# A 64-head long-convolution kernel on one core: outer-product tables, a new prologue, transposes ahead of the projection, and the projection in fp32r high and low parts

## The chip, the cores and the metric

The kernel runs on one core of a Trainium2 chip. A core has TensorE (matrix products, PE in the profile, its weight loads PEld), VectorE (DVE), ScalarE (ACT), GpSimd (POOL) and SyncE (SP, here the issuer of most transfers). Each engine works through its own instruction stream in order, and semaphores tie the streams together. The metric is the device time of one execution in microseconds; the median of several runs counts.

## What is computed

The input x is [128, 64, 1024]: batch, head, position. Cut to what matters:

```python
mask = arange(1024) < length[:, None]             # one length per batch row
u    = x * mask[:, None, :]
K    = 2 * einsum('hn,hnl->hl', Cs, exp(dtA[:, :, None] * arange(1024))).real   # 64 complex modes a head
y    = causal_convolution(u, K) + u * D[:, None]  # written as rfft * rfft -> irfft
y    = y * mask[:, None, :]
logits = einsum('bsd,ed->bse', y, route_w)        # 8 experts
h      = einsum('bsd,erd->bser', y, A)            # rank 16 each
out    = x + einsum('bser,eor->bso', top1_gate(logits)[..., None] * h, Bw)
```

Here s of the second half is the head (64 of them) and d the position (1024), so each head is one [128 x 1024] row block that is convolved, projected to 8 + 128 numbers, gated with the largest logit, and projected up again to 1024.

## The kernel before

Each head's 1024 positions are 8 blocks of 128, split into even and odd ones. One pass per head on TensorE is: `bring` (L1016, 6 fp32r matmuls of 384 columns into psS, which give the states that each block hands on), `project` of the head before (L1004, 8 fp32 matmuls of 136 columns into psZ, logits and rank-16 products together; the profile shows each fp32 matmul as two), `turn_x` of the head ahead (L991, 8 transposes), `inputs` two heads ahead (L1029, 2 fp32 matmuls), `within` (L1050, 9 fp32r matmuls of 512 columns, the convolution inside a pair of blocks), in whose middle stands `turn_wh` (L1074, one transpose of the gated products), `turn_k` (a transpose), `from_states` (L1064, 6 fp32r of 384 columns) and `up` of the head before (L1080, 6 fp32r of 512 columns).

[...] To keep accuracy each operand is cut into a high part (a copy by ScalarE, names ending in hi) and a low part (the difference, by VectorE or GpSimd, names ending in lo), and `three` (L981) adds high x high, low x high and high x low.

On the other engines, one head in the steady part:

- VectorE: `carry` (two scans `brought` with a final `Sf` each), then for the head before `top`, `rank`, `best`, `gate`, `wh` (the first largest logit, and the products times it; top, rank and wh read psZ in PSUM), with `frac` and `fraction` of the head three ahead in between, then `x_lo`, `b_lo`, `w_lo`, `whole` (four heads ahead), `cut` twice (Y is psY times the mask), and `add` twice (out is psO plus x).
- GpSimd: `s_lo`, `x_lo` (even half), two multiplications `wave` and `Grev` that make the decay-times-sine table of a head, `t_lo`, `g_lo`, and `frac` (L419).
- ScalarE: copies out of PSUM, high parts, and per head two angle tables (`turns`, L517 and L519) and one sine (L525) over 256 positions.
- The kernel's time response K goes to DRAM as a row (`krow`) and comes back skewed as a Toeplitz tile (`Traw`).

`run_steps` writes the steps i = 0 to 64 out on every engine; step i works on head i, and on i-1, i+1, up to i+4. What stands before that loop on each engine is the prologue: parameter maths on 64 partitions, transposes of tables and weights, and the tables of the first heads. There is no scheduler: the order on an engine is the order in the text. The gate chain and its reader are the lines that the prediction follows most:

```python
dve.reduce_max(top, psZ[:, 0:E])                              # L817
dve.scalar_tensor_tensor(rank, psZ[:, 0:E], top, desc, ...)   # L822
dve.reduce_max(best, rank)                                    # L827
dve.tensor_scalar(gate, rank, best, top, ...)                 # L833
dve.tensor_tensor(wh, psZ[:, E:NW], gate (broadcast), mult)   # L839
```

## Time and profile before

| | us |
|---|---|
| median of 3 runs | 622.37 |
| lowest and highest | 622.35, 623.7 |
| the profiled execution, whole | 623.93 |
| its span (first to last instruction) | 622.1 |
| mean granted TensorE clock | 0.992 |

The page lists busy time by engine, slices of the span, queues, the chain that ended last, and the costliest groups of instructions. A timeline lists instructions in order with start and duration; where a count stands, several are merged. An "idle before" in brackets names what the engine waited for. Matmuls are pipelined: their durations overlap, so what one costs is the distance between starts.

### The profile page before, as it was taken

What the parts mean: (1) busy time and instruction counts of PE and PEld (TensorE: products, weight loads), DVE (VectorE), ACT (ScalarE), POOL (GpSimd) and SP (SyncE); (2) the same over time, 40 slices, a digit from 0 to 9 for tenths busy, and PEclk for the clock granted to TensorE, in tenths of its full rate; (3) what the DMA queues carried; (4) which work ended last, traced back from release to release, by engine and by line L of the source; (5) the groups of instructions that cost most, each with busy time, mean ns of one, the idle gap of its engine ahead of it and who ended that gap; (6) DMA issues with size and microseconds to landing.
All of it is one profiled execution on the core that took longest, in us unless ns stands there. A gap on an engine that the chain in (4) does not pass through costs nothing.

```text
span 622.1 us, 13886 instructions
## 1 busy us (share of the span) xinstructions
PE 591.5 (95%) x3681; PEld 530.9 (85%) x3681; DVE 542.5 (87%) x1436; ACT 379.3 (61%) x1164; POOL 372.9 (60%) x474
## 2 busy tenths in 40 slices
PE   3379999999999999999999999999999999999995
PEld 2268998999899889988998998899899989988984
DVE  7778889988988898899889888988998898889874
ACT  3676656766676666567666766665676667666520
POOL 4465566557656755675576567556755765676520
PEclk9989999999999999999999999999999999999998
DMA  6023534453454345435534543454345345434521
GB/s 137 17 56 108 152 110 128 147 150 96 142 149 132 113 139 153 112 126 146 152 96 139 151 133 110 141 152 114 125 146 152 98 136 151 139 105 140 154 78 67
DMA packets 37074, 77.68 MB, mean 125 GB/s; under 512 B 11836, under 2 KB 20350, under 8 KB 36998
## 3 DMA queue, kind: packets, MB, share of 16 engines
q1 hardware_dynamic: 27846, 43.76, 29.5%
q10 hardware_dynamic: 9152, 33.03, 13.0%
q8 instruction: 32, 0.52, 0.4%
q14 instruction: 44, 0.36, 0.2%
HBM read 43.16 MB, written 33.62 MB: 123 GB/s over the span
## 4 chain that ended last, share of the span: by engine, by line
PE 92%; DVE 4%; issue 2%; POOL 1%; ACT 0%; DMA 0%; POOLq 0%
PE psYo L987 19%; PE psZ L1009 19%; PE psO L987 15%; PE psYe L987 12%; PE psS L987 11%; PE psO L1036 5%; PE psXe L1000 4%; PE psXo L1000 4%; PE psZ L1078 1%; PE psS L1047 1%; DMA logs<-in_L_cond_log_dt_dram 0%; DVE ex L693 0%; POOL Grev L436 0%; POOL wave L426 0%; DVE fraction L803 0%
## 5 line engine op out<-in xcount | busy, mean ns | idle before, releaser
L468 POOL TENSOR_TENSOR Slo<-Sf,Shi 128x384 fp32r<-128x384 f32 x64 | 64.9, 1015 | 210.1 <-ACT Shi L590 210.1
L852 DVE SCALAR_TENSOR_TENSOR brought<-Sf,tab,psS 64x128 f32<-64x128 f32 x256 | 89.0, 348 | 47.3 <-ACT Sf L585 40.9
L1009 PE MATMUL psZ<-Wt,Y 128*128 128x136 f32 x1024 | 129.6, 280 | 0.0
L1009 PEld LDWEIGHTS psZ<-Wt,Y 128*128 128x128 f32 x1024 | 127.8, 191 | 0.1
L531 ACT ACTIVATE Ghi<-Grev 128x256 fp32r<-128x256 f32 x64 | 26.8, 418 | 94.2 <-POOL Grev L436 94.2
L884 DVE TENSOR_TENSOR ost<-psO,xt 128x512 f32<-128x512 f32 x128 | 82.0, 676 | 2.2 <-PE psO L987 2.2
L461 POOL TENSOR_TENSOR Xlo<-xeven,Xhi 128x512 fp32r<-128x512 f32 x64 | 82.8, 1293 | 0.0
L568 ACT ACTIVATE Xhi<-psXe 128x512 fp32r<-128x512 f32 x64 | 38.2, 597 | 38.3 <-PE psXe L1000 38.3
L789 DVE TENSOR_SCALAR whole<-turns_t 128x256 f32<-128x256 f32 x64 | 57.8, 903 | 4.1 <-ACT turns_t L519 4.1
L585 ACT ACTIVATE Sf<-psS 128x128 f32<-128x128 f32 x64 | 17.7, 277 | 66.4 <-PE psS L987 66.4
L987 PE MATMUL psYo<-Xhi,Thi 128*128 128x512 f32 x128 | 55.6, 434 | 0.0
L987 PE MATMUL psO<-Bw_hi,whi 128*128 128x512 f32 x128 | 50.9, 397 | 0.7 <-ACT whi L595 0.7
L987 PE MATMUL psO<-Bw_lo,whi 128*128 128x512 f32 x128 | 51.4, 401 | 0.0
L987 PE MATMUL psO<-Bw_hi,wlo 128*128 128x512 f32 x128 | 51.2, 400 | 0.0
L987 PE MATMUL psYo<-Xhi,Tlo 128*128 128x512 f32 x128 | 50.8, 397 | 0.0
L987 PE MATMUL psYo<-Xlo,Thi 128*128 128x512 f32 x128 | 50.6, 395 | 0.0
L436 POOL TENSOR_TENSOR Grev<-wave,magQ 128x256 f32<-128x256 f32 x64 | 47.4, 741 | 5.0
L856 DVE SCALAR_TENSOR_TENSOR Sf<-Sf,tab,brought 128x128 f32<-128x128 f32 x128 | 45.0, 352 | 4.5
L419 POOL TENSOR_TENSOR frac<-whole,turns_h 128x256 f32<-128x256 f32 x64 | 46.6, 728 | 3.3 <-DVE whole L789 3.3
L446 POOL TENSOR_TENSOR Glo<-Grev,Ghi 128x256 fp32r<-128x256 f32 x64 | 46.9, 733 | 1.4 <-ACT Ghi L531 1.4
L453 POOL TENSOR_TENSOR Tlo<-Traw,Thi 128x256 fp32r<-128x256 f32 x64 | 46.9, 734 | 0.5 <-ACT Thi L562 0.5
L875 DVE TENSOR_TENSOR Y<-psYe,mask 128x512 f32<-128x512 f32 x64 | 43.5, 679 | 2.7 <-PE psYe L987 2.7
(194 smaller groups left out, 1670.8 us busy)
## 6 DMA issues: line engine op xcount, KB each, us to landing
xt<-in_x_dram SPq DMA_DIRECT2D x64, 512.0 KB, 4.1
out_dram<-ost ACTq DMA_DIRECT2D x63, 512.0 KB, 4.8
Traw<-kdram SPq DMA_DIRECT2D x64, 128.0 KB, 2.9
kdram<-krow SPq DMA_DIRECT2D x64, 1.0 KB
A_nat<-in_L_ffn_A_dram SPq DMA_DIRECT2D x1, 512.0 KB, 4.9
B_nat<-in_L_ffn_Bw_dram SPq DMA_DIRECT2D x8, 64.0 KB, 3.6
out_dram<-ost SPq DMA_DIRECT2D x2, 256.0 KB, 2.0
lens_i<-in_itok_B_dram SPq DMA_DIRECT2D x1, 64.0 KB, 3.6
```

The costliest lines, as they stand in the source:

```text
L419: pool.tensor_tensor(frac1[h.s2][:, :], whole[h.s2][:, :], turns_h[h.s2][:, :], ALU.subtract).then_inc(frac1_done, 1)
L436: pool.tensor_tensor(Grev[h.s2][:, :].rearrange("p (a b) -> p a b", b=G16), wave1[:, :].rearrange("p (a b) -> p a b", b=G16), magQ[:, h.n: ...
L446: pool.tensor_tensor(Glo[h.s4][:, :], Grev[h.s2][:, ::-1], Ghi[h.s4][:, :].bitcast(F32), ALU.subtract).then_inc(glo_done, 1)
L453: pool.tensor_tensor(Tlo[h.s2][:, :, :].rearrange("p a b -> p (a b)"), Traw[h.s2][:, ::-1], Thi[h.s2][:, :, :].rearrange("p a b -> p (a b) ...
L461: pool.tensor_tensor(Xlo[h.s2][:, 0, :], xeven[:, :], Xhi[h.s2][:, 0, :].bitcast(F32), ALU.subtract).then_inc(xlo_even, 1)
L468: pool.tensor_tensor(Slo[h.s2][:, :], Sf[h.s2][:, :], Shi[h.s2][:, :].bitcast(F32), ALU.subtract).then_inc(slo_done, 1)
L789: dve.tensor_scalar(whole[h.s2][:, :], turns_t[h.s2][:, :], ROUND, ROUND, ALU.add, ALU.subtract).then_inc(whole_done, 1)
L852: dve.scalar_tensor_tensor(brought[to, :], Sf[h.s2][fr, old], tab2[fr, BR, h.n:h.n + 1], psS[to, new], ALU.mult, ALU.add).then_inc(brought ...
L884: dve.tensor_tensor(ost[h.s2][:, half], psO[j][:, :], xt[h.s4][:, half], ALU.add).then_inc(added, 1)
L987: mm = pe.matmul(dst, a, b, start=first and i == 0, stop=last and i == n - 1, skip_group_check=True)
L1000: last = pe.transpose(psX[j][:, c * P:(c + 1) * P], xt[h.s4][:, at:at + P], ident[:, :])
L1009: last = pe.matmul(psZ[:, 0:NW], Y[:, j, c, :], Wt[:, 2 * c + j, :], start=(j == 0 and c == 0), stop=(j == 1 and c == NE - 1), skip_group_ ...
```

## The change

1. **Projection.** Before: 8 fp32 matmuls of 136 columns, stationary Y, moving Wt. After: ScalarE makes Yhi (two copies of 512 columns), VectorE makes the even Ylo and GpSimd the odd one; TensorE does 8 fp32r matmuls of 272 columns (Yhi times high and low weights side by side) and 8 of 136 columns (Ylo times high weights). The two halves of the result must be added: ScalarE copies the right half to `zlow`, VectorE adds it to `z` in SBUF, and top, rank and wh now read `z` in SBUF instead of psZ in PSUM.
2. **Order.** `turn_x` and `inputs` come before `project`; `turn_wh` comes after all of `within` and `turn_k` instead of in the middle of `within`.
3. **Tables.** Before, each head had its own 256-position angle, fraction and sine. After, one sine pass makes 16 coarse and 16 fine values for a group of heads (4, 12, 16, 16, 16 heads), and each head's table is the real part of a complex outer product: one GpSimd multiplication over 512 columns (`both`) and one addition (`Grev`). Angle steps, turns, fractions, sines, weighing and mirroring are done once a group, inside single steps ahead of it.
4. **Prologue.** Head 0 is done before the loop, which now starts at step 1; the transfers and inputs of head 2 are there too; the exponents move from GpSimd to VectorE; magnitudes of the first 4 heads are made apart from the rest; and a GpSimd order of its own is written out up to step 1.

The core of the diff, with line numbers left out:

```diff
-            def project(h, j):
-                need(pe, y_masked, h.n * 2 + j + 1)
-                for c in range(NE):
-                    last = pe.matmul(psZ[:, 0:NW], Y[:, j, c, :], Wt[:, 2 * c + j, :], ...)
+            def project(h):
+                need(pe, wlo_done, h.n)
+                for j in range(2):
+                    need(pe, yhi_done, h.n * 2 + j + 1)
+                    for c in range(NE):
+                        pe.matmul(psZ[:, 0:2 * NW], Yhi[:, j, c, :],
+                                  Whl[:, 2 * c + j, :, :].rearrange("p t w -> p (t w)"), ...)
+                for j in range(2):
+                    need(pe, *((ylo_odd, h.n + 1) if j else (ylo_even, h.n + 1)))
+                    for c in range(NE):
+                        last = pe.matmul(psZ[:, 0:NW], Ylo[:, j, c, :], Whl[:, 2 * c + j, 0, :], ...)
...
+            def z_low(h):                       # ScalarE
+                need(act, z_mm, h.n + 1)
+                act.activation(zlow[:, :], psZ[:, NW:2 * NW], ACT.Copy).then_inc(zlow_done, 1)
+            def y_hi(h, j):                     # ScalarE
+                need(act, y_masked, h.n * 2 + j + 1)
+                act.activation(Yhi[:, j, :, :], Y[:, j, :, :], ACT.Copy).then_inc(yhi_done, 1)
+            def joined(h):                      # VectorE
+                need(dve, zlow_done, h.n + 1)
+                dve.tensor_tensor(z[:, :], psZ[:, 0:NW], zlow[:, :], ALU.add)
...
-                dve.reduce_max(top[:, :], psZ[:, 0:E], axis=AX.X).then_inc(top_done, 1)
+                dve.reduce_max(top[:, :], z[:, 0:E], axis=AX.X).then_inc(top_done, 1)
-                dve.scalar_tensor_tensor(rank[:, :], psZ[:, 0:E], top[:, :], desc[:, :],
+                dve.scalar_tensor_tensor(rank[:, :], z[:, 0:E], top[:, :], desc[:, :],
-                                  psZ[:, E:NW].rearrange("p (e r) -> p e r", r=R),
+                                  z[:, E:NW].rearrange("p (e r) -> p e r", r=R),
...
+            def y_lo(h):                        # VectorE: even half; GpSimd has the same for the odd
+                need(dve, yhi_done, h.n * 2 + 1)
+                dve.tensor_tensor(Ylo[:, 0, ...], Y[:, 0, ...], Yhi[:, 0, ...].bitcast(F32), ALU.subtract)
...
             def g_table(h):                     # GpSimd
-                pool.tensor_tensor(wave1, wave[h.s2], magP[h] (broadcast), ALU.mult)      # 256
-                pool.tensor_tensor(Grev[h.s2], wave1, magQ[h] (broadcast), ALU.mult)      # 256
+                pool.tensor_tensor(both, coarse[h] (broadcast), fine[h] (broadcast), ALU.mult)  # 512
+                pool.tensor_tensor(Grev[h.s2], both[:, 0], both[:, 1], ALU.add)           # 256
...
             def step(head):                     # GpSimd
-                if head(0).there and not is_head(head(0), 0):
+                if head(-1).there:
+                    y_lo(head(-1))
+                if head(3).there and not is_head(head(0), 1):
+                    g_table(head(3))
+                if head(0).there:
                     s_lo(head(0))
                 if head(1).there:
                     x_lo(head(1))
...
                 if head(3).there:
                     g_lo(head(3))
-                if head(4).there:
-                    turn_parts(head(4))
+                if part_at(head(10)):
+                    angle_steps(part_at(head(10)))
+                if part_at(head(8)):
+                    turn_parts(part_at(head(8)))
+                if part_at(head(5)):
+                    weigh(part_at(head(5)))
```

How the instruction streams stand. TensorE in one steady step before, from the last matmul of `bring` to where `within` is cut by `turn_wh` (L987 is the helper `three`):

```order
L987 MATMUL psS<-Xhi,Blo 128x384
L1009 MATMUL psZ<-Wt,Y 128x136 x8
L1000 MATMUL psXe<-ident,xt 128x128 x4
L1000 MATMUL psXo<-ident,xt 128x128 x4
L1036 MATMUL psO<-Mx,Grev 128x129 x2
L987 MATMUL psYe<-Xhi,Thi 128x512
L987 MATMUL psYe<-Xlo,Thi 128x512
L987 MATMUL psYe<-Xhi,Tlo 128x512
L987 MATMUL psYo<-Xhi,Thi 128x512
L987 MATMUL psYo<-Xlo,Thi 128x512
L987 MATMUL psYo<-Xhi,Tlo 128x512
L1078 MATMUL psZ<-ident,wh 128x128
```

The projection comes first, and wh's transpose waits in the middle of `within`.

After, TensorE from the second row of transposes to the first matmul of `within` (L1147 and L1153 are the two kinds of projection matmul, L1125 is now `three`):

```order
L1136 MATMUL psXe<-ident,xt 128x128 x4
L1136 MATMUL psXo<-ident,xt 128x128 x4
L1179 MATMUL psO<-Mx,Grev 128x129 x2
L1147 MATMUL psZ<-Whl,Yhi 128x272 x8
L1153 MATMUL psZ<-Whl,Ylo 128x136 x8
L1125 MATMUL psYe<-Xhi,Thi 128x512
```

Nothing but these two projection rows stands between `inputs` and `within` now. And further on in the same step, from the last three matmuls of `within` to the first of `from_states`:

```order
L1125 MATMUL psYo<-Xhi,Thi 128x512
L1125 MATMUL psYo<-Xlo,Thi 128x512
L1125 MATMUL psYo<-Xhi,Tlo 128x512
L1191 MATMUL psS<-ident,kcol 2x128
L1218 MATMUL psZ<-ident,wh 128x128
L1125 MATMUL psYe<-Shi,Ghi 128x384
```

The transpose of wh has moved from the sixth matmul of `within` to behind its ninth and `turn_k`.

VectorE in one steady step before, from the end of `carry` to `whole`:

```order
L856 SCALAR_TENSOR_TENSOR Sf<-Sf,tab,brought 128x128
L817 TENSOR_REDUCE top<-psZ 128x1
L796 SCALAR_TENSOR_TENSOR frac<-egrid,tab,frac_1 128x256
L822 SCALAR_TENSOR_TENSOR rank<-psZ,top,desc 128x8
L803 TENSOR_SCALAR fraction<-frac 128x256
L827 TENSOR_REDUCE best<-rank 128x1
L833 TENSOR_SCALAR gate<-rank,best,top 128x8
L839 TENSOR_TENSOR wh<-psZ,gate 128x128
L810 TENSOR_TENSOR Xlo<-psXo,Xhi 128x512
L862 TENSOR_TENSOR Blo<-psO,Bhi 128x256
L868 TENSOR_TENSOR wlo<-psZ,whi 128x128
L789 TENSOR_SCALAR whole<-turns_t 128x256
```

This is one head's gate chain with the table work of others in between. After, VectorE across the edge between two steps, from `cut` (Y) and the two adds (ost) to the first part of `carry`:

```order
L1003 TENSOR_TENSOR Y<-psYe,mask 128x512
L1003 TENSOR_TENSOR Y<-psYo,mask 128x512
L1012 TENSOR_TENSOR ost<-psO,xt 128x512 x2
L1019 TENSOR_TENSOR Ylo<-Y,Yhi 128x512
L979 SCALAR_TENSOR_TENSOR brought<-Sf,tab,psS 64x128 x2
L983 SCALAR_TENSOR_TENSOR Sf<-Sf,tab,brought 128x128
```

Ylo has come in between the adds and the next step's carry. Further on in that step, from `x_lo` over the new z to `b_lo`:

```order
L931 TENSOR_TENSOR Xlo<-psXo,Xhi 128x512
L938 TENSOR_TENSOR z<-psZ,zlow 128x136
L944 TENSOR_REDUCE top<-z 128x1
L949 SCALAR_TENSOR_TENSOR rank<-z,top,desc 128x8
L954 TENSOR_REDUCE best<-rank 128x1
L960 TENSOR_SCALAR gate<-rank,best,top 128x8
L966 TENSOR_TENSOR wh<-z,gate 128x128
L989 TENSOR_TENSOR Blo<-psO,Bhi 128x256
```

The per-head frac, fraction and whole are gone from between these, and the gate chain reads z.

GpSimd in one steady step before:

```order
L461 TENSOR_TENSOR Xlo<-xeven,Xhi 128x512
L426 TENSOR_TENSOR wave<-wave,magP 128x256
L436 TENSOR_TENSOR Grev<-wave,magQ 128x256
L453 TENSOR_TENSOR Tlo<-Traw,Thi 128x256
L446 TENSOR_TENSOR Glo<-Grev,Ghi 128x256
L419 TENSOR_TENSOR frac_1<-whole,turns_h 128x256
L468 TENSOR_TENSOR Slo<-Sf,Shi 128x384
```

Slo, the last row, opens the next step.

GpSimd after:

```order
L452 TENSOR_TENSOR Ylo<-Y,Yhi 128x512
L488 TENSOR_TENSOR both<-coarse,fine 128x512
L498 TENSOR_TENSOR Grev<-both 128x256
L527 TENSOR_TENSOR Slo<-Sf,Shi 128x384
L520 TENSOR_TENSOR Xlo<-xeven,Xhi 128x512
L512 TENSOR_TENSOR Tlo<-Traw,Thi 128x256
L505 TENSOR_TENSOR Glo<-Grev,Ghi 128x256
```

The odd Ylo and the table of the head three ahead are first, and Slo, Xlo, Tlo, Glo are in one row behind them.

## Rows read from the trace of the kernel before

**Rows 1.** Section 1 of the page: engine, busy us, share of the span, instructions.
```profile
PE 591.5 (95%) x3681; PEld 530.9 (85%) x3681; DVE 542.5 (87%) x1436; ACT 379.3 (61%) x1164; POOL 372.9 (60%) x474
```

**Rows 2.** Busy time in one head's stretch, instructions, granted clock, DMA share, GB/s.
```profile
305.56:314.55 8.99, 8.99 (x59) 8.12 (x58) 8.09 (x22) 5.77 (x19) 5.70 (x8) 1.00 0.45 134
```

**Rows 3.** Timeline, TensorE, the same head: start, us, line, out<-in, shapes, count.
```profile
305.56 0.34 PE L987 MATMUL psS<-Xhi,Bhi 128*128 128x384 f32 x1
...
306.61 2.01 PE L1009 MATMUL psZ<-Wt,Y 128*128 128x136 f32 x16
308.46 0.60 PE L1000 MATMUL psXe<-ident,xt 128*128 128x128 f32 x4
...
313.15 0.39 PE L987 MATMUL psO<-Bw_hi,whi 128*128 128x512 f32 x1
...
314.55 0.34 PE L987 MATMUL psS<-Xhi,Bhi 128*128 128x384 f32 x1
```

**Rows 4.** Instructions by form, TensorE weight loads: count, busy us, mean ns.
```profile
L1009 PEld LDWEIGHTS psZ<-Wt,Y 128*128 128x128 f32 x1024 | 127.8, 191 | 0.1
...
L987 PEld LDWEIGHTS psO<-Bw_hi,whi 128*128 128x128 f32 x128 | 24.2, 189 | 4.1 <-ACT whi L595 0.9
```

**Rows 5.** Timeline, VectorE, one head in the steady part.
```profile
300.43 0.17 DVE L817 TENSOR_REDUCE top<-psZ 128x1 f32<-128x8 f32 x1
...
300.90 0.22 DVE L822 SCALAR_TENSOR_TENSOR rank<-psZ,top,desc 128x8 f32<-128x8 f32 x1
...
301.24 0.15 DVE L827 TENSOR_REDUCE best<-rank 128x1 f32<-128x8 f32 x1
301.43 0.29 DVE L833 TENSOR_SCALAR gate<-rank,best,top 128x8 f32<-128x8 f32 x1
301.75 0.29 DVE L839 TENSOR_TENSOR wh<-psZ,gate 128x128 f32<-128x128 f32 x1
...
303.15 0.95 DVE L789 TENSOR_SCALAR whole<-turns_t 128x256 f32<-128x256 f32 x1
...
305.22 1.27 DVE L884 TENSOR_TENSOR ost<-psO,xt 128x512 f32<-128x512 f32 x2
307.12 0.73 DVE L852 SCALAR_TENSOR_TENSOR brought<-Sf,tab,psS 64x128 f32<-64x128 f32 x2 [0.63 <-ACT Sf L585]
307.88 0.35 DVE L856 SCALAR_TENSOR_TENSOR Sf<-Sf,tab,brought 128x128 f32<-128x128 f32 x1
```

**Rows 6.** Timeline, GpSimd, the same head.
```profile
301.68 1.02 POOL L468 TENSOR_TENSOR Slo<-Sf,Shi 128x384 fp32r<-128x384 f32 x1 [3.25 <-ACT Shi L590]
302.66 1.29 POOL L461 TENSOR_TENSOR Xlo<-xeven,Xhi 128x512 fp32r<-128x512 f32 x1
303.91 0.67 POOL L426 TENSOR_TENSOR wave<-wave,magP 128x256 f32<-128x256 f32 x1
```

**Rows 7.** VectorE's `whole`, all 64: min/median/max ns, first and last start.
```profile
L789 DVE TENSOR_SCALAR whole<-turns_t x64: 275/951/962, 17.3 to 573.2; 128x256 f32<-128x256 f32 x64
```

**Rows 8.** Timeline near the end, VectorE's gate.
```profile
606.88 0.96 DVE L833 TENSOR_SCALAR gate<-rank,best,top 128x8 f32<-128x8 f32 x1
```

**Rows 9.** Timeline near the end, GpSimd at that time.
```profile
606.83 0.99 POOL L468 TENSOR_TENSOR Slo<-Sf,Shi 128x384 fp32r<-128x384 f32 x1 [5.16 <-ACT Shi L590]
```

**Rows 10.** Timeline of the prologue, VectorE.
```profile
18.38 1.39 DVE L934 TENSOR_TENSOR prod<-CA,Lm 64x128 f32<-64x128 f32 x1
```

**Rows 11.** Timeline of the prologue, GpSimd.
```profile
15.33 1.05 POOL L271 TENSOR_TENSOR rho<-tab,grid 128x512 f32<-128x512 f32 x1
...
18.37 1.26 POOL L461 TENSOR_TENSOR Xlo<-xeven,Xhi 128x512 fp32r<-128x512 f32 x1
```

**Rows 12.** Timeline, ScalarE, the steady head.
```profile
301.08 0.53 ACT L590 ACTIVATE Shi<-Sf 128x384 fp32r<-128x384 f32 x1
```

**Rows 13.** Timeline, TensorE, end of the prologue.
```profile
42.98 0.66 PE L987 MATMUL psS<-Xhi,Bhi 128*128 128x384 f32 x1 [1.27 <-ACT krow L556]
...
45.04 2.55 PE L1009 MATMUL psZ<-Wt,Y 128*128 128x136 f32 x16
```

More of the change, by code:

```diff
@@ L262, in __init__, with part_at @@
                 self.there = 0 <= n < H
+        class Part:
+            def __init__(self, k, start, stop):
+                self.k = k
+                self.start = start
+                self.n = stop - start
+                self.heads = slice(start, stop)
+        EDGES = [0, FIRST] + list(range(G16, H + 1, G16))
+        parts = [Part(k, EDGES[k], EDGES[k + 1]) for k in range(len(EDGES) - 1)]
+        def part_at(h):
+            for part in parts[2:]:
+                if part.start == h.n:
+                    return part
+            return None
         def is_head(h, *numbers):
@@ L475, in step @@
                     x_lo(head(1))
-                if head(3).there:
+                if head(3).there and is_head(head(0), 1):
                     g_table(head(3))
@@ new lines, in mirror @@
+            def mirror(part):
+                need(act, weighed, part.k * 3 + 3)
+                top, low = slice(0, N), slice(N, P)
+                for table, to, half, fr, scale in ((coarse, low, 1, top, 1.0), (coarse, top, 1, low, -1.0),
+                                                   (fine, low, 0, top, 1.0), (fine, top, 1, low, 1.0)):
+                    act.activation(table[to, half, part.heads, :], table[fr, half if table is fine else 0, part.heads, :],
+                                   ACT.Copy, scale=scale).then_inc(mirrored, 1)
@@ L1096, in step @@
                     bring(head(0))
-                if head(-1).there:
-                    project(head(-1), 0)
-                    project(head(-1), 1)
                 if head(1).there:
@@ L1153, in _ @@
                     last.then_inc(b_turned, 1)
+            pe.wait_ge(pack2_done, 2)
+            pe.wait_ge(xeven_done, 1)
+            turn_tables(pack2, psX[0], 5)
+            inputs(first[0])
+            turn_k(first[0])
+            bring(first[0])
+            turn_x(first[1], 0)
+            turn_x(first[1], 1)
             inputs(first[1])
             turn_k(first[1])
-            pe.wait_ge(w_done, 3)
+            within(first[0], 0)
+            within(first[0], 1)
+            inputs(first[2])
+            from_states(first[0])
+            turn_k(first[2])
             run_steps(step)
```

457 lines of the change are left out of this document (266 added, 191 removed).

## The prediction

> **What bounds the kernel now.** The page's first section comes first: TensorE is busy for 95% of the span [rows 1]. The windows view of one head in the steady part says the same more sharply: 8.99 us, TensorE busy for all of it at a granted clock of 1.00, VectorE for 8.09, GpSimd for 5.70 [rows 2]. The timeline gives TensorE's price list, by distances between starts [rows 3]: six fp32r matmuls of 384 columns take 306.61 - 305.56 = 1.05 us (0.175 each), six of 512 columns 314.55 - 313.15 = 1.40 (0.233 each, 0.456 ns a column), the projection 308.46 - 306.61 = 1.85 (16 instructions of 0.1156). One head is 314.55 - 305.56 = 8.99. So before, any us taken from TensorE's list in a step would count 64 times, and nothing else does, as long as the others arrive in time. What the reader should see besides is when the others work: GpSimd's row of work starts at 301.68 with Slo and runs on without a gap [rows 6], and VectorE's gate chain lies just before it, 300.43 to 302.04 [rows 5].
>
> **A hold between VectorE and GpSimd.** `whole` takes 275 ns at best and 951 ns in the median [rows 7]. The one in the timeline starts at 303.15, while GpSimd's Xlo runs from 302.66 to 303.95, and ends at 304.10, 0.15 us after it [rows 5, 6]. The gate, 0.29 us in the steady part [rows 5], once takes 0.96: 606.88 to 607.84, beside GpSimd's Slo, 606.83 to 607.82 [rows 8, 9]. A tensor_tensor with both inputs in SBUF takes 1.39 us for 128 elements, 18.38 to 19.77, beside GpSimd's Xlo, 18.37 to 19.63 [rows 10, 11]. But `wh`, which reads PSUM, takes 0.29 at 301.75 although Slo has begun [rows 5, 6]. I read: a VectorE instruction that takes its tensors from SBUF alone waits for the end of the GpSimd instruction that is under way; one that reads PSUM does not. The next GpSimd instruction then starts right behind. The kernel before pays this once a head, under slack.
>
> The Trainium skill (SBUF — State Buffer, section on the two separate sides) says that VectorE in a 2-port mode or with two SBUF inputs and GpSimd share a port pair as an exclusive lock, held for a whole instruction. The trace agrees (0.951 against 0.275 us). The rule speaks against this change: by it each step of the new kernel has rank, gate, wh and Ylo behind the lock, and without it the sum below would stay near 630.
>
> **The projection on TensorE.** Removed: 1.85 us a head. Added: 8 x 272 columns x 0.456 = 0.99, and 8 fp32r matmuls of 136 columns, which the trace does not show. Bounds: in proportion to columns 0.062 each, as a 512-column one 0.233. I take 0.11, because each needs its own weight load: an fp32r load lasts 189 ns and an fp32 load 191 [rows 4], so they look alike, and fp32 loads follow each other every 0.1156 us. 8 x 0.11 = 0.88, together 1.87. TensorE's list goes from 8.99 to 9.01: no gain, and -0.4 or +1.0 a head at the bounds.
>
> **The gate chain.** wh must now be there when `within` and `turn_k` are done, not in the middle of `within`, but project ends only before `within` too. With t = 0 at the first matmul of bring: bring 1.05, transposes and inputs to 2.36 (8.99 less all the rest), project to 4.24, `within` 9 x 0.233 and turn_k to 6.46. z is there at 4.37. Without any hold: copy of zlow 0.36 with its signals, the addition 0.33, top, rank, best, gate, wh about 1.3 (0.17 + 0.22 + 0.15 + 0.29 + 0.29 and 0.04 between [rows 5]): 6.36, and 0.12 to the transpose. That is just in time. With the hold it is not, because the chain now lies beside GpSimd's row. rank and wh read z from SBUF; GpSimd's order is Ylo, both, Grev, then Slo, Xlo, Tlo, Glo in one row as soon as Shi is there, which is when carry ends, about the time at which z comes. So gate waits for the end of Xlo, and wh for the end of Tlo.
>
> **The new period.** TensorE then waits for wh, and the period closes over a loop, each term from a row:
> - second add, half of 1.27 and a signal: 0.68 [rows 5]
> - VectorE's Ylo, new, before the carry: GpSimd's odd Ylo started with it, 1.29 as Xlo, so 0.62 of it are left, then its own 512 elements (the held 128 took 0.14 past the release [rows 10, 11], so 0.56) and 0.06: 1.24
> - carry, twice (307.88 - 307.12) + 0.35, and a signal: 2.26 [rows 5]
> - Shi: 0.57 [rows 12]
> - Slo 1.02 and Xlo 1.29, up to the gate's end: 2.33 [rows 6]
> - Tlo, 256 columns, as 0.67 [rows 6], and 0.14 for wh: 0.81
> - signal 0.14, transpose 0.11, from_states 1.05, up 1.40, results 0.14: 2.84 [rows 3]
>
> Sum 10.73, so +1.7 a head. The zlow copy, the addition and X fall out of it: they end while the gate is held anyway. GpSimd's `both` (512 columns with two repeated inputs, like rho, 1.05 [rows 11]; at most 1.29 as Xlo) hides before Slo; at 1.29 it pushes on the loop by about 0.2. ScalarE's two Yhi copies (Shi's 0.53 for 384 columns [rows 12] makes 0.6 for 512) stand in its wait for the cuts; the removed angle tables and sine freed as much.
>
> **Tables once per 16 heads.** Per head this takes frac, fraction, whole off VectorE, all hidden before: no gain by itself. Three groups are made in the steady part, with a `whole` of 512, two frac and a fraction in three steps in front of wlo, which has 0.4 us of room: 0.5 to 2 a group, plus GpSimd's steps: 5 in all. ScalarE's four turns and four mirrors (2 us) stand in its wait for the late wh.
>
> **Prologue and end.** Step 1 starts at 42.98, and the first project, 45.04 to 47.4, takes 2.55 us, a part of it at the lower clock [rows 13]. After, the first heads' tables are smaller, but GpSimd has to do 20.8 us of listed work between the first mirror (about 21) and the first odd Ylo (4 x 1.8 for tables, 2 Xlo 2.6, Glo and Tlo 6 x 0.73, steps and weighing 3.3, Slo 1.0, turn parts 1.0, Ylo 1.3), and VectorE's masks are held on its way. The first project ends at 42.5 to 46.5: -3 (between -5 and +1). At the end the last Yhi, Ylo, zlow and z stand open: +2.5.
>
> **Sum.** Span 622.1 + 62 x 1.7 (105.4) + 5 - 3 + 2.5 = 732. The median of the runs (622.37) lies 0.3 above the profile's span and 1.6 below the profiled execution, so the span's scale is kept: **732 us**. With `both` at 1.29 it is 745, with fewer of the four holds effective 700.
>
> **Rivals.**
> 1. *No hold where I see one.* GpSimd may drift so that the chain finds gaps, or rank and wh may not be held. Then TensorE's list decides: 9.01 and 0.05 of late wh a head (+4), groups +5, end +1.5, prologue -3: 630. For it: the steady rows show only one held VectorE instruction a head. Against: before, the SBUF ones lie in GpSimd's idle 3.25 us [rows 6].
> 2. *Faster.* The narrow fp32r matmul costs 0.062, not 0.11, and nothing holds. TensorE's list becomes 8.63, VectorE's own round with Ylo in it decides near 8.88: 62 x -0.11 = -7, +5, +1.5, -3: 619. It decides from the point where wh arrives before 6.1. Inside the loop of 10.73 a cheap narrow matmul gives nothing. The Trainium skill (TensorE: Matmul & The Clock Gate, section on weight-path modes) says that weights load faster when there are 128 of them and the type is not fp32; by it the 0.062 would be right. Rows 4 show no such difference for fp32r (189 against 191 ns).
> 3. *The reductions are held too.* top now reads SBUF, as best does; no row shows a reduction beside GpSimd work. One more boundary, about 1.1 a head: 800.
> 4. *TensorE's clock falls or the narrow matmul is 0.233.* TensorE idles 1.7 of 10.7 us. With a part at the lower clock (1.2 GHz) the first project took 2.55 for 1.85 [rows 3, 13]; such a stretch behind every wait would be +2 a head: 855; the dear matmul +0.9: 790.
>
> **How the numbers follow.** Forecast (700 to 765) 0.60, rival 1 0.14, rival 2 0.07, rival 3 0.08, rival 4 0.05, only some of the holds or a wash (621 to 700) 0.06. The range must take in rivals 1 and 3: 628 to 805, leaving out rivals 2 and most of 4. About 0.3% (1.9 us) is what a measurement can tell from no change; faster 0.07, within 0.03, slower 0.90.
>
> **What would show it.** Right: one period of 10.5 to 11 us in the steady timeline; TensorE idle about 1.7 us before the transpose of wh, released by VectorE; gate near 1.0, wh near 0.8 and Ylo near 1.2 us where 0.29, 0.29 and 0.7 are their free prices; the eight narrow matmuls 0.11 apart. Wrong: gate at 0.29 and TensorE busy throughout, or a wait of TensorE elsewhere, or a narrow matmul that is not 0.11. If TensorE's busy share stays at 95%, the whole argument on the hold has failed.

## The result, and the profile after

| | before | changed |
|---|---|---|
| median, us | 623.04 | 750.39 |
| lowest and highest | 622.35, 624.09 | 749.1, 750.83 |
| span of the profiled execution | 622.1 | 748.9 |
| mean granted TensorE clock | 0.992 | 0.978 |

The changed kernel takes 1.204 times as long (95% interval 1.201 to 1.207). The forecast was 732, range 628 to 805.

The page of the changed kernel, section 1 and the first line of section 4; they answer to [rows 1]:

```profile
PE 615.9 (82%) x3681; PEld 539.8 (72%) x3681; DVE 666.7 (89%) x1393; ACT 395.9 (53%) x1214; POOL 483.5 (65%) x507
...
DVE 56%; PE 25%; issue 12%; ACT 4%; POOL 1%; ACTq 0%; DMA 0%; DVEq 0%; POOLq 0%
```

TensorE has fallen from 95% to 82%, and VectorE holds 56% of the chain that ended last. Groups of instructions (count | busy us, mean ns | idle us before them and what ended it):

```profile
L1218 PE MATMUL psZ<-ident,wh 128*128 128x128 f32 x64 | 21.2, 332 | 100.7 <-DVE wh L966 100.7
...
L1019 DVE TENSOR_TENSOR Ylo<-Y,Yhi 128x512 fp32r<-128x512 f32 x64 | 84.4, 1318 | 0.0
L960 DVE TENSOR_SCALAR gate<-rank,best,top 128x8 f32<-128x8 f32 x64 | 62.4, 975 | 2.6 <-DVE best L954 0.3
L966 DVE TENSOR_TENSOR wh<-z,gate 128x128 f32<-128x128 f32 x64 | 48.7, 760 | 2.2
L949 DVE SCALAR_TENSOR_TENSOR rank<-z,top,desc 128x8 f32<-128x8 f32 x64 | 24.1, 376 | 2.3
L954 DVE TENSOR_REDUCE best<-rank 128x1 f32<-128x8 f32 x64 | 10.3, 161 | 2.2
L944 DVE TENSOR_REDUCE top<-z 128x1 f32<-128x8 f32 x64 | 10.3, 161 | 2.4
```

TensorE waits 100.7 us in front of the 64 transposes of wh, and hardly anywhere else once the prologue is over. gate, on eight numbers a row, costs 975 ns where 290 is its free price [rows 5]. One step in the timeline, first VectorE, then GpSimd, then TensorE:

```profile
303.32 0.16 DVE L944 TENSOR_REDUCE top<-z 128x1 f32<-128x8 f32 x1
303.51 0.38 DVE L949 SCALAR_TENSOR_TENSOR rank<-z,top,desc 128x8 f32<-128x8 f32 x1
303.93 0.16 DVE L954 TENSOR_REDUCE best<-rank 128x1 f32<-128x8 f32 x1
304.12 0.99 DVE L960 TENSOR_SCALAR gate<-rank,best,top 128x8 f32<-128x8 f32 x1
305.15 0.77 DVE L966 TENSOR_TENSOR wh<-z,gate 128x128 f32<-128x128 f32 x1
...
309.41 1.36 DVE L1019 TENSOR_TENSOR Ylo<-Y,Yhi 128x512 fp32r<-128x512 f32 x1
```

```profile
302.85 1.01 POOL L527 TENSOR_TENSOR Slo<-Sf,Shi 128x384 fp32r<-128x384 f32 x1 [1.19 <-ACT Shi L682]
303.82 1.27 POOL L520 TENSOR_TENSOR Xlo<-xeven,Xhi 128x512 fp32r<-128x512 f32 x1
305.05 0.73 POOL L512 TENSOR_TENSOR Tlo<-Traw,Thi 128x256 fp32r<-128x256 f32 x1
...
308.94 1.28 POOL L452 TENSOR_TENSOR Ylo<-Y,Yhi 128x512 fp32r<-128x512 f32 x1 [0.76 <-ACT Yhi L699]
310.18 1.51 POOL L488 TENSOR_TENSOR both<-coarse,fine 128x512 f32<-128x512 f32 x1
```

```profile
304.14 0.27 PE L1191 MATMUL psS<-ident,kcol 128*2 128x128 f32 x1
305.98 0.33 PE L1218 MATMUL psZ<-ident,wh 128*128 128x128 f32 x1 [1.56 <-DVE wh L966]
...
310.89 1.25 PE L1147 MATMUL psZ<-Whl,Yhi 128*128 128x272 f32 x8
311.98 1.01 PE L1153 MATMUL psZ<-Whl,Ylo 128*128 128x136 f32 x8
312.82 0.44 PE L1125 MATMUL psYe<-Xhi,Thi 128*128 128x512 f32 x1
```

Read the ends side by side: rank ends at 303.89, Slo at 303.86; gate at 305.11, Xlo at 305.09; wh at 305.92, Tlo at 305.78; VectorE's Ylo at 310.77, 0.55 us after GpSimd's. So each of the held VectorE instructions ends at, or at most 0.14 us behind, the end of a GpSimd instruction (0.55 for Ylo, whose own 512 elements come after the wait). The two reductions (0.16) run through. It works the other way too: `both` starts at 310.18, while VectorE's Ylo runs, and takes 1.51 us; in the prologue, at 39.19 with VectorE idle, it takes 1.06.

The span grew by 126.8 us. The distance from the first transpose of wh to the last is 564.8 us before and 686.0 after (+121.2: 62 steps of 10.84 instead of 9.00 make 114.1, what the steps around the three groups of tables take above 10.84 makes 6.0, and the last step, 7.94 instead of 6.70, makes 1.2); the first transpose comes at 55.44 instead of 50.15 (+5.3); behind the last one lie 7.5 instead of 7.2 (+0.3).

The granted clock was not 1.00 throughout the steady part. Three times (330.3 to 333.6, 494.2 to 497.4 and about 723 to 726 us) it was 0.50, the lower of its two levels (1.2 GHz). Here are the same two matmuls of `up` in the second group's step and in the first group's:

```profile
331.34 0.63 PE L1125 MATMUL psO<-Bw_hi,whi 128*128 128x512 f32 x1
331.76 0.63 PE L1125 MATMUL psO<-Bw_lo,whi 128*128 128x512 f32 x1
```

```profile
156.14 0.40 PE L1125 MATMUL psO<-Bw_hi,whi 128*128 128x512 f32 x1
156.37 0.40 PE L1125 MATMUL psO<-Bw_lo,whi 128*128 128x512 f32 x1
```

They lie 0.42 us apart instead of 0.23. TensorE had idled the same in both steps (1.63 and 0.68 us in one, 1.64 and 0.69 in the other), yet the clock fell in one of them only. That step takes 12.84 us where its like in the first group takes 11.81, and a step of the third group takes 12.20 where its like takes 11.20: of the 6.0 us, 4.0 are group work and 2.0 the clock.

### The profile page after: what moved, and what is told of

Same layout as the page of the kernel before. It is cut to its first block, busy times and chain, and to the rows that moved or that the text cites. A ratio compares the mean times of both kernels' runs of the same rounds, so it can differ in the third digit from the quotient of the medians.

```text
span 748.9 us, 13962 instructions
## 1 busy us (share of the span) xinstructions
PE 615.9 (82%) x3681; PEld 539.8 (72%) x3681; DVE 666.7 (89%) x1393; ACT 395.9 (53%) x1214; POOL 483.5 (65%) x507
## 3 DMA queue, kind: packets, MB, share of 16 engines
q10 hardware_dynamic: 9152, 33.03, 10.8%
## 4 chain that ended last, share of the span: by engine, by line
DVE 56%; PE 25%; issue 12%; ACT 4%; POOL 1%; ACTq 0%; DMA 0%; DVEq 0%; POOLq 0%
PE psO L1125 12%; DVE brought L979 12%; DVE Ylo L1019 11%; DVE gate L960 8%; DVE wh L966 6%; DVE Sf L983 6%; PE psYo L1125 4%; PE psYe L1125 4%; DVE rank L949 3%; DVE z L938 3%; PE psZ L1218 3%; ACT zlow L693 2%; DVE top L944 1%; DVE best L954 1%; DVE ost L1012 1%
## 5 line engine op out<-in xcount | busy, mean ns | idle before, releaser
L452 POOL TENSOR_TENSOR Ylo<-Y,Yhi 128x512 fp32r<-128x512 f32 x64 | 82.8, 1294 | 140.5 <-ACT Yhi L699 140.5
L699 ACT ACTIVATE Yhi<-Y 128x512 fp32r<-128x512 f32 x128 | 78.7, 632 | 55.0 <-DVE Y L1003 55.0
L1218 PE MATMUL psZ<-ident,wh 128*128 128x128 f32 x64 | 21.2, 332 | 100.7 <-DVE wh L966 100.7
L488 POOL TENSOR_TENSOR both<-coarse,fine 128x512 f32<-128x512 f32 x64 | 93.4, 1460 | 1.2 <-ACT fine L616 1.2
L1019 DVE TENSOR_TENSOR Ylo<-Y,Yhi 128x512 fp32r<-128x512 f32 x64 | 84.4, 1318 | 0.0
L1147 PE MATMUL psZ<-Whl,Yhi 128*128 128x272 f32 x512 | 79.8, 298 | 0.0
L1153 PE MATMUL psZ<-Whl,Ylo 128*128 128x136 f32 x512 | 65.3, 270 | 4.8 <-POOL Ylo L452 3.5
L1147 PEld LDWEIGHTS psZ<-Whl,Yhi 128*128 128x128 f32 x512 | 67.8, 189 | 0.1
L1153 PEld LDWEIGHTS psZ<-Whl,Ylo 128*128 128x128 f32 x512 | 63.4, 192 | 5.4 <-POOL Ylo L452 3.6
L960 DVE TENSOR_SCALAR gate<-rank,best,top 128x8 f32<-128x8 f32 x64 | 62.4, 975 | 2.6 <-DVE best L954 0.3
L682 ACT ACTIVATE Shi<-Sf 128x384 fp32r<-128x384 f32 x64 | 33.7, 526 | 52.3 <-DVE Sf L983 52.3
L1125 PE MATMUL psO<-Bw_hi,whi 128*128 128x512 f32 x128 | 52.6, 411 | 3.0 <-ACT whi L687 2.8
L1125 PE MATMUL psO<-Bw_lo,whi 128*128 128x512 f32 x128 | 52.3, 409 | 0.0
L1125 PE MATMUL psO<-Bw_hi,wlo 128*128 128x512 f32 x128 | 51.9, 405 | 0.0
L1125 PE MATMUL psYo<-Xhi,Thi 128*128 128x512 f32 x128 | 51.6, 403 | 0.0
```

What stands on the lines that cost most here:

```text
L452: pool.tensor_tensor(Ylo[:, 1, :, :].rearrange("p a b -> p (a b)"), Y[:, 1, :, :].rearrange("p a b -> p (a b)"), Yhi[:, 1, :, :].rearrange ...
L488: pool.tensor_tensor(both[:, :, :, :], coarse[:, :, h.n, :].rearrange("p t (a b) -> p t a b", b=1).to_broadcast(wide), fine[:, :, h.n, :]. ...
L699: act.activation(Yhi[:, j, :, :], Y[:, j, :, :], ACT.Copy).then_inc(yhi_done, 1)
L960: dve.tensor_scalar(gate[:, :], rank[:, :], best[:, :], top[:, :], ALU.is_equal, ALU.mult).then_inc(gate_done, 1)
L1019: dve.tensor_tensor(Ylo[:, 0, :, :].rearrange("p a b -> p (a b)"), Y[:, 0, :, :].rearrange("p a b -> p (a b)"), Yhi[:, 0, :, :].rearrange( ...
L1125: mm = pe.matmul(dst, a, b, start=first and i == 0, stop=last and i == n - 1, skip_group_check=True)
```

## The experiments

The theory is the hold: VectorE's instructions with all tensors in SBUF, other than the reductions, wait for the end of the GpSimd instruction under way. This puts wh late, and each step then lasts as long as the loop of 10.8 us that runs from wh over the adds, Ylo and the carry to the next wh. Its main rival is a chain that is merely longer by the zlow copy, the addition and Ylo. Other rivals put the cost into the order or the tables. "us a head" below is the distance between two transposes of wh in steps without group work. The kernels build on each other: e2 on e1, e5 to e8 on e2, e9 on e8, e11 and e12 on e10. e6, e10, e11 and e12 do the third pass of the projection in bf16.

### e1: z and rank in PSUM

```diff
-        z = sb("z", [P, NW])
-        rank = sb("rank", [P, E])
+        z = psZ[:, 0:NW]
+        rank = psZ[:, 2 * NW:2 * NW + E]
```

> The changed kernel with two buffers put elsewhere: z and rank lie in PSUM (in psZ's own bank) and no longer in SBUF, so the addition, top, rank, best, gate and wh all have a PSUM operand. No instruction is added, dropped or moved. Changed kernel for comparison: 750.4 us, period 10.84 us, gate 0.99, wh 0.76, VectorE's Ylo 1.36. Theory (hold: a VectorE instruction whose tensors are all in SBUF waits for the end of the GpSimd instruction under way): gate and wh fall to about 0.3 each, Ylo stays held at 1.3. Transpose of wh to next carry 4.82, carry to z 3.03, z to the end of wh 1.65, signal 0.14: period 9.64, time 750.4 - 63 x 1.2 = 675. Rival A (the chain is merely longer by the zlow copy, the addition and Ylo, and would be as late without a hold): gate and wh change little or TensorE's wait stays, 740 to 755. Rival B (GpSimd's row itself is what the step waits for): gate is short, but TensorE waits elsewhere, period above 10.4, 725 or more.

Measured: 668.3 us, ratio to before 1.073 (1.071 to 1.075); 9.52 us a head (expected 9.64 and 675 us). Groups of e1, the same instructions:

```profile
L1019 DVE TENSOR_TENSOR Ylo<-Y,Yhi 128x512 fp32r<-128x512 f32 x64 | 83.3, 1302 | 0.0
...
L966 DVE TENSOR_TENSOR wh<-psZ,gate 128x128 f32<-128x128 f32 x64 | 18.6, 291 | 2.3
...
L960 DVE TENSOR_SCALAR gate<-psZ,best,top 128x8 f32<-128x8 f32 x64 | 18.2, 284 | 2.6 <-DVE best L954 0.3
L949 DVE SCALAR_TENSOR_TENSOR psZ<-psZ,top,desc 128x8 f32<-128x8 f32 x64 | 15.0, 234 | 2.2
```

And gate stands beside the same GpSimd instruction as it did in the changed kernel (timeline of e1, VectorE, then GpSimd):

```profile
207.17 0.28 DVE L960 TENSOR_SCALAR gate<-psZ,best,top 128x8 f32<-128x8 f32 x1
```

```profile
207.00 1.28 POOL L520 TENSOR_TENSOR Xlo<-xeven,Xhi 128x512 fp32r<-128x512 f32 x1
```

So 82 us have gone by moving two small tensors, with every instruction and its place in the order unchanged: rivals A and B fall. It isn't that SBUF operands cost more by themselves either: in the changed kernel's own last steps, with rank in SBUF and GpSimd idle, gate takes 0.29 (at 732.78).

### e2: the even Y in PSUM too

```diff
-  Y[:, 0] = psY[0] * mask ; Ylo[:, 0] = Y[:, 0] - Yhi[:, 0]
+  psY[0]  = psY[0] * mask ; Ylo[:, 0] = psY[0]  - Yhi[:, 0]
```

> As the run before, and in addition the even half of the cut result Y stays in PSUM (written in place into psYe), so VectorE's Ylo reads PSUM too. Same instructions, same order. Theory (hold): Ylo falls from 1.36 to about 0.7, period 9.64 - 0.66 = 8.98, which is TensorE's own list (9.03), so the period is 9.0 to 9.1 and the time 750.4 - 63 x 1.78 = 638; what is left above the kernel before is the prologue (5.3 us measured in the trace) and the group steps (6 us). Rival A (longer chain, no hold): no change against the changed kernel, 740 to 755. Rival C (Ylo hides beside GpSimd's odd Ylo anyway, since project needs both halves): Ylo is short but the period stays as in the run before, 9.6, 675.

Measured: 645.6 us, ratio 1.036 (1.034 to 1.038); 9.06 a head, Ylo 680 ns. The edit also adds one wait, of `within` for the Ylo that reads psYe. The period is as the theory has it, and the chain with all its new members fits beside TensorE's list of 9.03. GpSimd's `both` now meets an Ylo that reads PSUM, and it gets its free price back. The changed kernel's page has the first row, that of e2 the second:

```profile
L488 POOL TENSOR_TENSOR both<-coarse,fine 128x512 f32<-128x512 f32 x64 | 93.4, 1460 | 1.2 <-ACT fine L616 1.2
```

```profile
L488 POOL TENSOR_TENSOR both<-coarse,fine 128x512 f32<-128x512 f32 x64 | 68.1, 1063 | 1.2 <-ACT fine L616 1.2
```

The time is 8 us above the 638, since a group of tables now costs 4.2 to 4.4 us (distances of the transposes of wh around the first one: 9.53, 9.50, 9.25, 9.86, 9.90, 9.86, 9.66, 9.26) and no longer 1.3, or 2.3 with the clock down. The slack beside a late wh had hidden the rest.

### e3: the fp32 projection back

```diff
-  Yhi x (Whi|Wlo), Ylo x Whi; zlow copy; z = psZ + zlow
+  pe.matmul(psZ[:, 0:NW], Y[:, j, c, :], Wt[:, 2 * c + j, :], ...)   # fp32, top, rank, wh read psZ
```

> The changed kernel with the projection alone undone: 8 fp32 matmuls of 136 columns on Y, no Yhi, Ylo, zlow, z and no low part of the weights; new tables, order and prologue stay. Theory (hold through the projection's new SBUF operands): wh reads PSUM and is short, rank too; only gate stays held, to the end of Xlo. Loop without Ylo (1.24) and without the wait for Tlo (0.46): 10.84 - 1.7 = 9.1, so 9.0 to 9.2 a head, 750.4 - 63 x 1.7 = 643; if the two group effects stay, 635 to 645. Rival D (the order of the steps, wh's transpose with nothing behind it, is what costs): the period stays above 10, 700 or more. Rival E (tables and GpSimd's 'both' of 1.5 us cost it): also above 10, and TensorE waits for Slo or Xlo and not for wh.

Measured: 635.2 us, ratio 1.019 (1.017 to 1.021); 9.00 a head, groups 3.2 each, first wh at 52.19. So tables, order and prologue together cost 12 of the 127 us, and the projection with its SBUF operands the rest. Rivals D and E fall. gate is the one instruction of the chain, reductions aside, that still has all its tensors in SBUF; its median is 394 ns and its highest 971.

### e4: the old order, held operands kept

```diff
-  bring, turn_x, inputs, project, within, turn_k, turn_wh
+  bring, project, turn_x, inputs, within (turn_wh in its middle), turn_k
```

(and with it, on VectorE, the gate chain ahead of Xlo, on ScalarE zlow ahead of Xhi)

> The changed kernel with the order alone undone: project stands right behind bring, turn_x and inputs after it, wh's transpose in the middle of within; on VectorE the gate chain stands before Xlo and on ScalarE the zlow copy before Xhi. All else as changed. Theory (hold): z is there about 1.4 us earlier, so gate and wh fall before or beside Slo alone; Ylo stays held (1.3). Loop: transpose to carry 4.8, carry 2.3, z to wh 1.65 with at most one hold of 0.7: 8.8 to 9.5, time 630 to 670, most likely period 9.3, 655. Rival A (longer chain, no hold): period 10.84 less 1.4 at most, 9.4, the same time, but with gate at 0.99 if that is its own price in the new form. Rival F (the order does not matter because Ylo comes too late for a project right behind bring): TensorE waits for Ylo before project, period 10.5, 725 or more.

Measured: 693.9 us, ratio 1.114 (1.112 to 1.116); 9.60 a head in the undisturbed steps. gate falls to 307 ns and wh to 321 with the operands still in SBUF, since they now lie in front of Slo, in the gap of GpSimd: the hold is a matter of who is beside whom. Ylo stays at 1319. By the period alone rival A (9.4) would fit as well; its gate of 0.99 doesn't. A group costs 6.9 to 8.9 us here. In the first one TensorE waits for whi 0.79 us behind the four turns, 1.41 behind the sine and 0.96 behind the mirrors, and 0.86 and 1.15 for GpSimd's Ylo. The 1.41 is a hold again: VectorE's `fraction`, all in SBUF, takes 1.56 beside GpSimd's Xlo (0.61 in the changed kernel at 153.49), and the sine waits for it. These waits were read, and none was removed by itself. So the time is above the 630 to 670 expected, and the period 0.1 above the upper end.

### e5: the prologue's late Ylo

```diff
+            y_lo(first[0])          # GpSimd, moved up from the start of step 1
             weigh(parts[1])
             g_lo(first[3])
-            y_lo(first[0])
```

> The kernel of e2_z_rank_y_in_psum (z, rank and even Y in PSUM; 645.6 us, first transpose of wh at 53.00) with one instruction moved: in GpSimd's prologue the odd Ylo of head 0 stands ahead of the weighing of the second group of tables, and no longer behind it and Glo of head 3. Theory P (the prologue's loss lies at the first projection, whose last four matmuls waited 3.42 us for that Ylo, which stood behind work that waits for a sine): the Ylo starts at 43.6 behind Glo, ends at 44.9, the first wh comes about 3.5 us earlier, at 49.4, and the time is 642. Rival (the low clock and the late carry of head 1 decide; the rest of step 1 is late anyway): the first wh moves by less than 1 us, the time by less than 1. Rival Q (the weighing is now late for the table of head 4): the gain at the first projection is given back within three steps, 645.

Measured: 647.4 us, ratio 1.039 (1.037 to 1.041), 1.8 above e2. Theory P fell as it was put: the first project did end 2.9 us earlier (`within` starts at 46.16 instead of 49.01), yet the first transpose of wh came at 53.76 instead of 53.00. ScalarE shows why (timeline of e5, ScalarE, then VectorE):

```profile
47.34 0.75 ACT L617 ACTIVATE coarse<-coarse 64x192 f32<-64x192 f32 x2 [1.60 <-POOL fine L480]
48.11 0.75 ACT L617 ACTIVATE fine<-fine 64x192 f32<-64x192 f32 x2
48.77 0.25 ACT L678 ACTIVATE Sf<-psS 128x128 f32<-128x128 f32 x1
```

```profile
49.05 0.73 DVE L981 SCALAR_TENSOR_TENSOR brought<-Sf,tab,psS 64x128 f32<-64x128 f32 x2 [3.99 <-ACT Sf L678]
```

The copy Sf, which the carry waits for, stands behind the mirror of the second group of tables, and the mirror waits for the weighing. So the same late work stood in front on two queues, and the edit moved it on one.

### e6: the low pass in bf16

```diff
-        Ylo = sb("Ylo", [P, 2, NE, P], F32R)
+        Ylo = sb("Ylo", [P, 2, NE, P], BF16)
+        Wb = sb("Wb", [P, NB, NW], BF16)     # copied once from the high weights
```

> The kernel of e2 with the third pass of the projection in bf16: Ylo is written as bf16 and multiplied with a bf16 copy of the high weights, made once in the prologue. Eight matmuls of 136 columns as before. It measures the price in dispute: does a narrow matmul cost its weight load (0.105 each in fp32r, 0.1156 in fp32) or its columns (136 x 0.456 ns = 0.062)? Theory of the prediction (weight loads look alike for all types): still 0.10 to 0.11 each, time 645.6. Rival 2 of the prediction as a mechanism (a 16-bit type loads its weights faster): 0.06 to 0.07 each, TensorE's list 9.03 - 0.34 = 8.69, but the loop over wh, carry and the gate chain of about 8.98 then sets the period: 9.00 instead of 9.06, time 641 to 643, TensorE waiting 0.3 for wh.

Measured: 644.2 us, ratio 1.034 (1.032 to 1.036). Weight loads of the two kinds of projection matmul in e6, and the stretch itself in the timeline:

```profile
L1154 PEld LDWEIGHTS psZ<-Whl,Yhi 128*128 128x128 f32 x512 | 67.9, 189 | 0.1
L1160 PEld LDWEIGHTS psZ<-Wb,Ylo 128*128 128x128 bf16 x512 | 30.2, 98 | 8.4 <-POOL Ylo L455 3.9 <-DVE Ylo L1023 1.1
```

```profile
301.54 0.65 PE L1160 MATMUL psZ<-Wb,Ylo 128*128 128x136 bf16 x8
301.99 0.48 PE L1131 MATMUL psYe<-Xhi,Thi 128*128 128x512 f32 x1
```

Eight take 0.45 us, 0.056 each; in fp32r they take 312.82 - 311.98 = 0.84, 0.105 each. The prediction's price (0.10 to 0.11 whatever the type) fell. The bf16 matmul costs about its columns (136 x 0.456 ns is 0.062). The fp32r one costs more than that, and the row that halves with the type is its weight load, 189 to 192 against 98 ns, so the load is the likely limit; both operands changed their type at once, so this is argued and not shown. The 0.39 us saved on TensorE's list turned into a wait for wh: in a quiet step turn_k starts at 237.99 and wh's transpose only at 238.41, and the period is still 9.06 (9.00 expected). So two limits lie side by side here. (The 1.0 us that the expectation of e10 speaks of was read in a step with group work.)

### e7: the old order with nothing held

The kernel of e2 with the diff of e4, and on ScalarE whi and krow ahead of the group work.

> The kernel of e2 with the order of before: project right behind bring, turn_x and inputs behind it, wh's transpose in the middle of within, gate chain ahead of Xlo on VectorE, the zlow copy ahead of Xhi and the whi copy ahead of the group work on ScalarE. Theory (with the holds gone and slack in the wh loop, TensorE's list decides, and group work on ScalarE hides behind whi): period 9.03 to 9.06 and groups 1 to 2 us each instead of 4.4: 645.6 - 8 = 636 to 640. Rival (project now waits for Ylo, which is there 0.5 us before it at best, so group work shows there instead): period 9.1 or more, groups as before, 645 or above. In e4_old_order the same order with the holds cost 9.60 a head.

Measured: 655.8 us, ratio 1.053 (1.051 to 1.055); 9.27 a head, so the forecast of 636 to 640 was wrong and the rival's side right. Its reason holds only around a group, where TensorE waits for GpSimd's Ylo (0.42, 0.19 and 0.78 us in the first one); in quiet steps it doesn't. There ScalarE copies zlow and both Xhi before Shi, so Shi starts at 301.33, 1.0 after the carry's end (300.32), Slo ends at 302.98, and from_states starts at 303.08. The order that suited the old projection doesn't suit the new one.

### e8: group work spread over 12 steps

```diff
-  angle_steps(head 10), turns(9), whole(8), turn_parts(8), fractions(7), clamp(6), sines(6), weigh(5), mirror(4)
+  angle_steps(15, 14), turns(14, 13), whole(12), turn_parts(11), fractions(10, 9), clamp(8), sines(7),
+  weigh(7, 6, 5), mirror(6, 5, 4)      # heads ahead; one or two instructions a step on each engine
```

> The kernel of e2 with the work of a table group spread over 12 steps instead of lying in 5: at most one or two of its instructions a step on each engine (angle steps 15 and 14 heads ahead, turns 14 and 13, whole 12, turn parts 11, the two fractions 10 and 9, clamp 8, sine and first weighing 7, the rest 6 to 4). Theory G (a group costs 4.4 us because four turns or four mirrors in a row stand in front of the whi copy on ScalarE, and two fractions in front of wlo on VectorE, more than the 0.9 and 0.45 us of room there): each step now fits into the room, a group costs 0.5 to 1 us, time 645.6 - 3 x 3.7 = 634. Rival (what costs is the total work, on an engine without any slack): no gain, 643 to 646.

Measured: 632.8 us, ratio 1.016 (1.014 to 1.017), 12.7 below e2. The steps around a group now all lie between 9.04 and 9.15 (one step of 9.74 stands alone near the end). Theory G stands: the same work costs at most 0.2 us a group in small pieces, and 4.2 to 4.4 in one.

### e9, e10: a shorter loop, in fp32r and in bf16

```diff
   DVE: carry
-       x_lo
        z, top, rank, best, gate, wh
+       x_lo
   ACT:
-       s_hi, z_low
+       z_low, s_hi
-  brought = Sf * tab + psS     # SBUF
+  psS     = Sf * tab + psS     # in place
```

> The kernel of e8_group_work_spread (632.8 us, 9.06 a head) with a shorter loop over wh: on VectorE the gate chain stands ahead of Xlo (0.69 us), on ScalarE the zlow copy ahead of Shi (0.53), and brought lies in PSUM (written in place into psS), so that no Sf can be held. The projection's low pass stays fp32r. Theory L (two limits lie side by side at 9.03 to 9.06: TensorE's list, and the loop wh, from_states, up, bring, carry, Xlo, gate chain, wh): shortening the loop alone gives nothing but its 0.03, time 631 to 633, and TensorE's wait before wh's transpose is gone. Rival (the loop alone is the limit): 8.7 a head, 612.

> As e9_shorter_loop_fp32r and the third pass of the projection in bf16 (as in e6_low_part_in_bf16, where eight narrow matmuls took 0.45 instead of 0.84 and the time moved by 1.3 us only, TensorE waiting 1.0 for wh instead). Theory L: now both limits are lower, TensorE's list 9.03 - 0.39 = 8.64, VectorE busy 8.5 of it, so 8.65 to 8.80 a head and 632.8 - 63 x 0.33 = 612 (606 to 617). Rival (VectorE, 8.5 us of work with its small waits, is the next limit): 8.95 or more, 626 or above.

Measured: e9 637.4 us, ratio 1.022 (1.020 to 1.024); e10 615.4, ratio 0.987 (0.985 to 0.990). Quiet steps: 9.06 and 8.71. With e6 these make a square: bf16 alone gives 0, the shorter loop alone 0, both together -0.35 us a head. e9 is even 4.6 above e8, which was not foreseen: 12 steps take 9.53 (one 9.72) instead of 9.06, those in which VectorE has whole, a fraction or the clamp in front of wlo. With Xlo moved behind wh the room there is gone; TensorE's `up` then waits for wlo (timeline of e9, VectorE, then TensorE):

```profile
119.94 0.55 DVE L933 TENSOR_SCALAR fraction<-frac 128x512 f32<-128x512 f32 x1
120.41 0.28 DVE L1004 TENSOR_TENSOR wlo<-psZ,whi 128x128 fp32r<-128x128 f32 x1
```

```profile
120.79 0.47 PE L1135 MATMUL psO<-Bw_hi,whi 128*128 128x512 f32 x1 [0.25 <-DVE wlo L1004]
```

### e11, e12: the prologue, and the group work once more

e11 makes the four moves that its expectation names. e12 puts the group work of VectorE between carry and z:

```diff
+                whole_turns, fractions, clamp      # of the group, if any in this step
                 joined(head(-1))
...
                 b_lo(head(2))
-                whole_turns, fractions, clamp
                 w_lo(head(-1))
```

> As e10_shorter_loop_bf16, with four moves in the prologue, each against a wait read in the trace: four of the eight masks on VectorE behind the first carry instead of ahead of it (they were held, 4.7 us for eight, and the carry came at 31.2 though its input was there at 29.3); on ScalarE Thi and kcol of the first heads ahead of Shi; the odd Ylo of head 0 ahead of the second weighing on GpSimd; and the sine, Ghi and mirror of the second group into step 1, behind the copies that bring and carry wait for (in e5 the Ylo alone gained nothing because Sf of head 1 stood behind the mirror). Theory: first transpose of wh at 47.5 to 49.5 instead of 53.4, time of e10 less 4 to 6 us. Rival (the low clock after the idle stretches gives the gain back): less than 2 us.

> The kernel of e11_loop_and_prologue (610.4 us) with VectorE's share of the group work (whole, two fractions, clamp, one instruction in each of four steps) standing between the carry and the addition z instead of ahead of wlo. In e11 exactly these four steps of a group took 9.17 instead of 8.71 us, twelve in all, 5.5 us. Theory: ahead of z VectorE waits 0.36 us for the zlow copy, so 0.5 us of work costs 0.15 there; the four steps come to 8.85 to 8.9, time 610.4 - 12 x 0.3 = 607. Rival H (the instructions have all tensors in SBUF and would now be held to the end of GpSimd's Grev, which ends 0.1 to 0.3 us before the carry does, or would hold up Slo): no gain or a loss, 610 to 613.

Measured: e11 610.4 us, ratio 0.979 (0.977 to 0.981), 5.1 below e10; the first transpose of wh is at 46.77, the second, 10.7 later, at 57.47 (before: 59.15). e12 605.5 us (607 expected), ratio 0.972 (0.970 to 0.973); the twelve steps are back at about 8.72, and rival H falls. Page and windows of e12:

```profile
PE 574.0 (95%) x3681; PEld 505.1 (84%) x3681; DVE 531.1 (88%) x1394; ACT 393.5 (65%) x1214; POOL 456.1 (76%) x507
```

```profile
300.00:400.00 100.00, 100.00 (x653) 88.49 (x651) 90.35 (x237) 67.38 (x211) 79.46 (x84) 1.00 0.45 139
```

In the second row TensorE is busy for all of the 100 us, at a step that is 0.29 shorter than before. e12 beats the kernel before by 2.8% with the change's own tables and split projection, once its low pass is in bf16, its operands lie in PSUM and nothing stands in front of what someone waits for.

## Why the prediction was right, and where not

- **The mechanism** was right: on TensorE's list alone the change was to gain nothing, and the hold is what made it +1.84 us a head. e1 and e2 took it away at two places and the period fell by 1.32 and 0.46.
- **The loop**, forecast 10.73, measured 10.84. By its terms in the timeline, with the forecast in brackets: second add and signal 0.61 (0.68), Ylo 1.39 (1.24), carry 2.30 (2.26), Shi 0.60 (0.57), Slo and Xlo to the gate's end 2.26 (2.33), to the end of wh 0.81 (0.81), signal to the results of up 2.88 (2.84). Ylo was the term mis-sized most: 0.55 past the end of GpSimd's was right (0.56), but 0.81 of that was still to run when VectorE came, not 0.62 (309.41 to 310.22).
- **TensorE's list**: a narrow matmul 0.105 (0.11 forecast), a wide one 0.136 (0.124); together 1.93 instead of 1.87. The loop hides it.
- **both**: taken as 1.05, at most 1.29. It took 1.51, since it waits for VectorE's Ylo. I had the hold in one direction only. It cost nothing: GpSimd is idle 1.19 before Slo, so the +0.2 that I set for a dear `both` was wrong as well.
- **Groups**: 5 forecast, 6.0 measured, near by luck. 2.0 of it is the lower clock in two steps, which the term did not have. The other 4.0 are less than the 5: the largest wait is 0.69 for whi behind the group's sine on ScalarE (at 155.36), and not the room of 0.4 before wlo. With wh on time the same work cost 13 us (e2), and hardly anything when it was spread (e8).
- **Prologue**: -3 forecast, bounds -5 and +1, measured +5.3. This step failed. I added up GpSimd's list and looked at no other queue. Up to bring of head 0 the new prologue is 5 us ahead (26.7 against 31.74). Then the eight masks, held, take 4.70 us (2.02 before), and the carry behind them starts 1.9 after its input is there; the prediction feared this and gave it no price. kcol of head 1 stands behind Shi of head 0 (TensorE waits 4.26); the last narrow matmuls wait 3.48 for the odd Ylo, and Sf of head 1 stands behind the mirror. e11 undid all of it and the first wh came 7.1 us earlier than in e10; 5.1 of them reached the end, since the next step was still 10.7 long.
- **End**: +2.5 forecast, +1.5 measured, 1.2 in the last step and 0.3 behind its transpose. The last Ylo and z stand open as said (TensorE waits 1.03 for Ylo and 2.01 for wh), but gate and wh are not held there.
- **Sum**: 62 x 0.11 = 6.8 for the loop's terms (10.84 for 10.73) and 62 x 0.03 = 1.9 because the sum took +1.7 a head where 10.73 is 1.73 above 9.00; with 1.0 (groups), 8.3 (prologue) and -1.0 (end) this is 17 us above 732, 749 for the span of 748.9. Half of the miss is the loop's 8.7, half the prologue. The median lies 1.5 above the span here, where the prediction took the two as equal.
- **Rivals**: 1 (no hold) and 3 (reductions held) fell, the latter by top and best at 161 ns. Rival 4 came true in small: the clock was at 0.50 in the prologue (from 35 to 40 us, behind 30 to 35 in which TensorE was busy for 0.82 of 5, and for a part of 50 to 55) and in three of the steady steps, which cost 2 us and not 2 a head; in the others, each with a wait of about 1.6, it stayed at 1.00. Its dear matmul fell with the 0.105. Rival 2 had the wrong type: fp32r weights load at the price of fp32 (189 to 192 ns), bf16 ones in 98. The Trainium skill (TensorE: Matmul & The Clock Gate, section on weight-path modes) lets weights load faster if the type is not fp32, 32 bits at a time. The rows agree with the second half (191 / 98 is 1.95 for a type of half the width); the prediction took the first half to include fp32r, and the rows show that it doesn't.
